# Windowed attention with 64 key columns for 32 queries, values moved by DMA, and half of the rotary sum on VectorE

## The chip, the cores and the metric

The kernel runs on one core of one Trainium2 chip. The metric is the device time of one execution in microseconds. Engines are named TensorE (PE in the profile; PEld is its weight load), VectorE (DVE), ScalarE (ACT), GpSimd (POOL) and SyncE (SP, which here only issues DMAs).

## What is computed

`x` has 32 sequences of 128 tokens with 128 channels. A causal attention with a linear bias (phase A) and a cross attention (phase B) come first; both lie outside the change. Then six layers follow, each a windowed attention and a gated MLP, both on token-shifted input. The attention's core, per layer and for 16 heads of 64:

```python
q = q * cos * scale + rotate_half(q) * sin * scale
k = k * cos * inv + rotate_half(k) * sin * inv
# local_attention, w = 32: a block of 32 queries sees its own and the previous block's keys
bk2, bv2 = (look(bk), look(bv))
mask = (it < jb) | (it > jb + w) | (jb == -1)
sim = jnp.einsum('bhwie,bhwje->bhwij', bq, bk2) * QK_SCALE
attn = jax.nn.softmax(jnp.where(mask, -jnp.finfo(sim.dtype).max, sim), -1)
out = jnp.einsum('bhwij,bhwje->bhwie', attn, bv2)
```

A block of 32 queries needs 64 keys, so the first 64 queries need keys 0 to 63, queries 64 to 95 keys 32 to 95, and queries 96 to 127 keys 64 to 127.

## The kernel before

The work of a layer's attention is cut into 128 groups, one for every 4 heads of a sequence. One step of the software pipeline takes in one group at one end and finishes an older one at the other; `LAG`-like numbers in the class `WIN` say how many steps behind its intake each stage of a group runs. Every engine runs a program of its own, written out in order, and waits on semaphores. `windowed` runs steps 5 to 15 of a layer unrolled, bodies 2 to 14 of eight steps (`STEPS`) in a hardware loop, and the last body unrolled. The first five steps (`FILL`) of a layer are laid between the last parts of the previous MLP, and eight drain steps of a layer between the first parts of its MLP.

The stages of a group and who runs them, before the change:

- Step 0: TensorE projects queries and keys (`win_project`, L701, through `split_product`, L698) into `proj_ps` and values (`win_values`, L715) into the upper half of `value_ps`. VectorE multiplies by the rotary tables (`win_cos` L1487, `win_sin` L1495), ScalarE squares (`win_square` L1043), VectorE sums squares (`win_norms` L1502) and clamps (`win_clamp` L1512). GpSimd adds `by_cos` and `by_sin` of queries and keys (`win_rotate` L1206). ScalarE copies the values to `vout` (L1063).
- Every second step GpSimd raises the norms of two groups to the power -1/2 (`win_rnorm` L1214) and, a step later, multiplies both groups' rotated tiles by them (`win_unit` L1226).
- Step 3: TensorE transposes queries and keys (`win_heads` L691), ScalarE copies them to `qk_t` (L1034).
- Step 5: TensorE writes the mask (L730) and adds the scores (`win_scores` L741) in one of two bank pairs, `win_ps`; a head's scores are 128 columns wide. VectorE takes row maxima (`win_max` L1519).
- Step 6: ScalarE takes four exponentials in place, with their row sums (L1052). VectorE takes reciprocals (`win_recip` L1527) and scales the probabilities into `prob` (`win_scale` L1537).
- Step 7: TensorE transposes the probabilities (L757), ScalarE copies them to `prob_t` (L1069), TensorE sums the values (`win_sum_values` L771) into the lower half of `value_ps`. ScalarE's copy to `vout` takes these sums and the new group's values together.
- Step 8: TensorE projects the sums out (L793); VectorE adds every fourth result to `y` (`win_add` L1544).

Every fourth step also brings in a sequence: VectorE's `win_tok` (L1463), TensorE's `win_input` (L672), ScalarE's `xt_high` (L1023) and VectorE's `win_split` to `xt_low` (L1469). The order on each engine within a step, before:

```python
# TensorE: project, turn_probs, values, mask, scores, sum_values, heads, project_out, (input)
# ScalarE: exponentials, copy_probs, square, copy_values, copy_heads, (xt_high)
# VectorE: cos, sin, recip, scale, max, norms, clamp, (tok), (xt_low), (add)
# GpSimd:  rotate, rnorm or unit
```

SyncE issues all DMAs in one order: in each layer the six chunks of `wqkv`, `shift_tokens` of the layer before (two DMAs for each of eight quads of sequences, L507 and L508, which feed the MLP), eight loads of `wo` (L522), then `w1` and `w2`. The MLP's first statistics on VectorE (`mlp_stats`, L1589) stand in the first drain step and wait for the first quad of `shift_tokens`.

## Time and profile before

| what | us |
|---|---|
| median of 3 runs (lowest, highest) | 4208.51 (4206.87, 4213.31) |
| the profiled execution, time | 4210.7 |
| the profiled execution, span | 4208.9 |
| TensorE busy | 3918.9 (93%) |
| VectorE busy | 3703.7 (88%) |
| ScalarE busy | 3550.0 (84%) |
| GpSimd busy | 3379.4 (80%) |
| DMA queue of SyncE, share of 16 engines | 3.3% |

Consecutive instructions of one engine overlap in the timeline: the distance between two starts, here called the pitch, is less than the first one's duration. A wait that an engine had is given in brackets behind the row, with the engine and line that ended it. The granted clock of TensorE over the span was 0.989 of full speed.

### The profile page before, as it was taken

How to read it: one execution, taken by the hardware profiler on the slowest of the kernel's cores; microseconds unless marked ns; L12 is line 12 of the kernel's file. 1: busy time of each engine (PE TensorE's matmuls, PEld its weight loads, DVE VectorE, ACT ScalarE, POOL GpSimd, SP SyncE). 2: the span in 40 equal slices, each digit the busy share in tenths (PEclk: the TensorE clock that was granted, in tenths of full speed). 3: DMA queues.
4: the chain of work that ended last, by engine and by line, in shares of the span. 5: the costliest groups of instructions: out<-in, count | busy, mean ns of one | idle time of the engine just before them, and what ended most of it. 6: DMA issues, size and time to landing. Idle time of an engine off the chain costs nothing.

```text
span 4208.9 us, 137255 instructions
## 1 busy us (share of the span) xinstructions
PE 3918.9 (93%) x49504; PEld 3102.0 (74%) x49504; DVE 3703.7 (88%) x8896; ACT 3550.0 (84%) x11595; POOL 3379.4 (80%) x2461
## 2 busy tenths in 40 slices
PE   7998885999999999989999999999899999999998
PEld 5666664777777777777777777777777777777776
DVE  7998887999988999979999889999799998899996
ACT  6888995999977999959999779999599997699995
POOL 4554446999978999969999789999599997799993
PEclk9999997999999999999999999999999999999999
DMA  3000000000000000010000000000100000000001
GB/s 84 0 0 1 0 0 16 3 2 0 0 21 22 5 0 0 1 41 4 2 0 0 15 28 5 0 0 1 41 4 2 0 0 13 15 5 0 0 1 36
DMA packets 81122, 38.89 MB, mean 9 GB/s; under 512 B 60084, under 2 KB 73266, under 8 KB 80946
## 3 DMA queue, kind: packets, MB, share of 16 engines
q1 hardware_dynamic: 80946, 36.56, 3.3%
q8 instruction: 108, 1.77, 0.2%
q14 instruction: 68, 0.56, 0.0%
HBM read 21.92 MB, written 2.10 MB: 6 GB/s over the span
## 4 chain that ended last, share of the span: by engine, by line
ACT 42%; PE 33%; DVE 13%; issue 10%; POOL 2%; ACTq 1%; SPq 0%; DMA 0%; DVEq 0%; POOLq 0%
ACT pair L1052 20%; PE bank L771 12%; ACT prob_t L1069 7%; ACT vout L1063 6%; ACT qk_t L1034 5%; PE bank L691 5%; PE pair L848 4%; PE bank L698 3%; DVE top L1443 3%; PE bank L793 2%; DVE qk_parts L1418 2%; PE bank L864 2%; PE bank L672 1%; DVE by_sin L1411 1%; ACT prob L977 1%
## 5 line engine op out<-in xcount | busy, mean ns | idle before, releaser
L1214 POOL TENSOR_TENSOR rnorm<-norm2g,neg_half 128x16 f32<-128x16 f32 x384 | 1115.3, 2905 | 181.7 <-DVE norm2g L1512 172.4
L1052 ACT ACTIVATE pair<-pair,top 128x128 f32<-128x128 f32 x3072 | 1055.8, 345 | 34.9 <-DVE top L1519 24.2
L1206 POOL TENSOR_TENSOR rotated<-by_cos,by_sin 128x512 f32<-128x512 f32 x768 | 985.8, 1284 | 51.0 <-DVE by_sin L1495 44.4
L1226 POOL TENSOR_TENSOR rotated<-rotated,rnorm 128x512 f32<-128x512 f32 x768 | 785.3, 1043 | 0.5
L698 PE MATMUL bank<-wqkv_high,xt_high 128*128 128x512 f32 (+1 forms) x1536 | 649.5, 423 | 15.9 <-ACT squares L1043 14.5
L1052 ACT ACTIVATION_READ_ACCUMULATOR pair<-pair,top 128x1 f32 x3072 | 652.3, 212 | 0.0
L1487 DVE TENSOR_TENSOR by_cos<-bank,rot_cos 128x512 f32<-128x512 f32 x768 | 529.9, 690 | 108.2 <-PE bank L698 91.5
L1063 ACT ACTIVATE vout<-bank 128x512 f32<-128x512 f32 (+1 forms) x810 | 466.0, 575 | 150.5 <-PE bank L771 145.1
L771 PE MATMUL bank<-prob_t,vout 128*32 128x128 f32 x12288 | 495.2, 279 | 94.0 <-ACT prob_t L1069 56.8
L1537 DVE TENSOR_TENSOR prob<-pair,rsum 128x512 f32<-128x512 f32 x768 | 530.9, 691 | 40.0
L1043 ACT ACTIVATE squares<-bank 128x512 f32<-128x512 f32 x768 | 458.8, 597 | 109.7 <-DVE by_sin L1495 92.0
L1502 DVE TENSOR_REDUCE norm<-squares 128x8 f32<-128x512 f32 x768 | 519.3, 676 | 11.3 <-ACT squares L1043 9.9
L1519 DVE TENSOR_REDUCE top<-pair 128x4 f32<-128x512 f32 x768 | 522.4, 680 | 0.7
L1495 DVE TENSOR_TENSOR by_sin<-bank,sin_now 128x512 f32<-128x512 f32 x768 | 522.4, 680 | 0.0
L698 PE MATMUL bank<-wqkv_low,xt_high 128*128 128x512 f32 (+1 forms) x1536 | 520.6, 339 | 0.0
L698 PE MATMUL bank<-wqkv_high,xt_low 128*128 128x512 f32 (+1 forms) x1536 | 520.1, 339 | 0.0
L1196 POOL TENSOR_TENSOR kz_parts<-qk_parts,cst 128x512 fp32r<-128x512 f32 x256 | 266.2, 1040 | 307.4 <-DVE qk_parts L1418 307.4
L691 PE MATMUL bank<-cst,rotated 128*128 128x128 f32 x3072 | 504.3, 287 | 2.7 <-POOL rotated L1226 2.5
L1069 ACT ACTIVATE prob_t<-bank 128x512 f32<-128x512 f32 x768 | 474.3, 618 | 4.8 <-PE bank L757 4.8
L793 PE MATMUL bank<-wo_sb,vout 128*128 128x128 f32 x3072 | 472.8, 276 | 2.0 <-ACT vout L1063 2.0
L771 PEld LDWEIGHTS bank<-prob_t,vout 128*32 128x32 f32 x12288 | 289.8, 109 | 239.6 <-ACT prob_t L1069 196.5
L757 PE MATMUL bank<-cst,prob 128*128 128x128 f32 x3072 | 461.8, 273 | 1.4 <-ACT qk_t L1034 1.4
(142 smaller groups left out, 8451.6 us busy)
## 6 DMA issues: line engine op xcount, KB each, us to landing
wqkv_sb<-in_L_ffn_Wqkv_dram SPq DMA_DIRECT2D x36, 256.0 KB, 4.0
ctx_all<-y SPq DMA_DIRECT2D x48, 128.0 KB
ctx_all<-y SPq DMA_DIRECT2D x48, 127.0 KB
wo_sb<-in_L_ffn_Wo_dram SPq DMA_DIRECT2D x48, 64.0 KB, 2.0
out_dram<-y SPq DMA_DIRECT2D x8, 256.0 KB, 3.5
w_sb<-in_L_ffn_W_dram SPq DMA_DIRECT2D x6, 341.0 KB, 3.0
w_sb<-in_L_ffn_W_dram SPq DMA_DIRECT2D x12, 64.0 KB
cst<-in_constants_dram SPq DMA_DIRECT2D x1, 582.0 KB, 3.9
```

The lines of the kernel that those rows point to most:

```text
L691: last = nc.tensor.transpose(turned_ps(it)[:, k * P:(k + 1) * P], flat[:, k * P:(k + 1) * P], ident)
L698: last = nc.tensor.matmul(dst, a[slot][:, :], w[:, which, cols], start=(n == 0), stop=(n == 2))
L771: last = nc.tensor.matmul(value_ps[PAD * h:PAD * (h + 1), half * P:(half + 1) * P], vout[jl][:, at:at + PAD], prob_t[jl % 2][:, h % 2 * 2 ...
L793: last = nc.tensor.matmul(acc_ps[:, 0:P], vout[(j - 1) % STEPS][:, half * P:(half + 1) * P], wo_sb[:, k * P:(k + 1) * P], start=(k == 0), ...
L1052: last = nc.scalar.activation(at, at, ACT.Exp, bias=top[jl % 2][:, h:h + 1], accum_out=psum_raw[jl % 2][:, h:h + 1])
L1063: nc.scalar.activation(vout[j][:, cols], value_ps[:, cols], ACT.Copy).then_inc(c_vout, 1)
L1069: nc.scalar.activation(prob_t[(j - WIN.probs) % 2][:, :, :].rearrange("k h q -> k (h q)"), turn_c_ps[:, :], ACT.Copy).then_inc(c_pt, 1)
L1206: nc.gpsimd.tensor_tensor(rotated[j % 4][:, :, :, :], by_cos[j % 2][:, :, :, :], by_sin[j % 2][:, :, :, :], ALU.add).then_inc(c_rot, 1)
L1214: nc.gpsimd.tensor_tensor(rnorm[slot][:, :, :].rearrange("t g n -> t (g n)"), norm2g[slot][:, :, :].rearrange("t g n -> t (g n)"), neg_hal ...
L1226: nc.gpsimd.tensor_tensor(at, at, rnorm[slot][:, i, :].unsqueeze(2).to_broadcast([P, 2 * HG, DH]), ALU.mult).then_inc(c_unit, 1)
L1487: nc.vector.tensor_tensor(by_cos[j % 2][:, :, :, :], got, table(rot_cos, layer).unsqueeze(2).to_broadcast([P, 2, HG, DH]), ALU.mult).then_ ...
L1537: nc.vector.tensor_tensor(prob[jl % 2][:, :, :].rearrange("q (e i) k -> q e i k", e=2), win_ps[jl % 2].rearrange("q e (i k) -> q e i k", i=2),
```

## The change

Keys: the four heads' scores of a group become 64 columns wide instead of 128, with three bases of keys for three blocks of queries, so scores, maxima, exponentials, scaling and transposes work on half the columns (two transposes for four). Value sums run on 64x64 tiles and need values of other tokens in their own half of the partitions; for these SyncE copies parts of `vout` into `vmoved`, four DMAs for every two groups. The transposed probabilities come out in the lower half of `value_ps` and are copied with the values; the sums go into free halves of the score banks and have a copy of their own. VectorE takes over the query half of the rotary sum. The lags `turn` and `exp` change, and the order of the stages on TensorE, ScalarE and VectorE. `wo` is loaded by one DMA, and `wqkv` of the next layer ahead of this layer's moves. Left out of the diff below: the constants of the mask, semaphores, and the parts of the drain and of the first steps that follow the new order.

```diff
+    turn = 4
     scores = 5
     top = 5
-    exp = 6
+    exp = 5
     scale = 6
     probs = 7
     value = 7
     out = 8
+KEYS = 2 * PAD
+BASES = (0, PAD, 2 * PAD)
...
-        win_ps = [t[:, :].rearrange("q (e n) -> q e n", e=2)[:, :, 0:2 * P] for t in (pair45, pair12)]
+        win_ps, sum_ps = [[t[:, :].rearrange("q (e n) -> q e n", e=2)[:, :, at:at + P] for t in (pair45, pair12)] for at in (0, P)]
...
+            def move_values(l, it, pair):
+                j = 2 * pair + 1
+                sp.wait_ge(c_vout, l * VOUTS + it * STEPS + j + 1)
+                if has(it * STEPS + j - STEPS):
+                    sp.wait_ge(c_value, l * GROUPS + it * STEPS + j - STEPS + 1)
+                elif l:
+                    sp.wait_ge(c_value, l * GROUPS)
+                for i, n, base in ((0, 0, BASES[1]), (0, 1, BASES[2]), (1, 0, BASES[0]), (1, 1, BASES[1])):
+                    sp.dma_start(vmoved[pair][i * KEYS:(i + 1) * KEYS, :, n, :],
+                                 vout_all[base:base + KEYS, 2 * pair:2 * pair + 2, (2 + i) * P:(3 + i) * P]).then_inc(c_moved[pair], 16)
+            def move_body(l, it, first=0):
+                for pair in range(first, STEPS // 2):
+                    move_values(l, it, pair)
...
-                for h in range(HG):
-                    for half in range(2):
-                        sp.dma_start(wo_sb[PAD * h:PAD * (h + 1), :].rearrange("r (g s c) -> r g s c", g=NG, s=2)[:, :, half, :],
-                                     wo[l].rearrange("(g h s r) c -> h s r g c", g=NG, h=HG, r=PAD)[h, half]).then_inc(s_wo_in, 16)
+                sp.dma_start(wo_sb[:, :].rearrange("r (k c) -> r k c", c=P), wo[l].rearrange("(k r) c -> r k c", r=P)).then_inc(s_wo_in, 16)
...
+                if l:
+                    for pair in range(2):
+                        move_values(l, 0, pair)
...
+                if l + 1 < DEPTH:
+                    load_wqkv(l + 1)
+                move_layer(l)
...
                     flat = rotated[jl % 4][:, :, :, :].rearrange("t a h d -> t (a h d)")
                     for k in range(4):
-                        last = nc.tensor.transpose(turned_ps(it)[:, k * P:(k + 1) * P], flat[:, k * P:(k + 1) * P], ident)
+                        if k == 3 and not isinstance(it, int):
+                            sums_ready(layer, it, j)
+                        last = nc.tensor.transpose(heads_ps[:, k * P:(k + 1) * P], flat[:, k * P:(k + 1) * P], ident)
...
                     jl = (j - WIN.scores) % STEPS
                     for i in range(2):
-                        for lower, keys in ((0, slice(0, DH)), (DH, slice(WINDOW, P))):
+                        for lower, n, base in ((0, DH, BASES[0]), (DH, PAD, BASES[1]), (DH + PAD, PAD, BASES[2])):
                             for e in range(2):
-                                rows, q0, k0 = slice(e * DH, (e + 1) * DH), i * P + lower, (2 + i) * P
-                                last = nc.tensor.matmul(win_ps[jl % 2][lower:lower + DH, e, i * P + keys.start:i * P + keys.stop],
-                                                        qk_t[jl % 4][rows, q0:q0 + DH], qk_t[jl % 4][rows, k0 + keys.start:k0 + keys.stop],
+                                rows, q0, k0 = slice(e * DH, (e + 1) * DH), i * P + lower, (2 + i) * P + base
+                                last = nc.tensor.matmul(win_ps[jl % 2][lower:lower + n, e, i * KEYS:(i + 1) * KEYS],
+                                                        qk_t[jl % 4][rows, q0:q0 + n], qk_t[jl % 4][rows, k0:k0 + KEYS],
                                                         start=False, stop=False, skip_group_check=True, tile_position=(e * DH, lower))
...
-                    for h in range(HG):
-                        last = nc.tensor.transpose(turn_c_ps[:, h * P:(h + 1) * P], prob[jl % 2][:, h, :], ident)
+                    for e in range(2):
+                        last = nc.tensor.transpose(value_ps[:, e * P:(e + 1) * P], prob[jl % 2][:, e, :], ident)
                     last.then_inc(c_pturn, 1)
...
+            def sums_ready(layer, it, j):
+                if here(it, j, WIN.value):
+                    jl = (j - WIN.value) % STEPS
+                    if jl % 2 == 0:
+                        pe.wait_ge(c_moved[jl // 2], 64 * (layer * ENDED + it + (1 if j >= WIN.value else 0)))
+                    if here(it, j, WIN.scale):
+                        pe.wait_ge(c_scaled, layer * GROUPS + it * STEPS + j - WIN.scale + 1)
+                    pe.wait_ge(c_vout, layer * VOUTS + it * STEPS + j + 1)
...
                 if here(it, j, WIN.value):
...
-                    for half in range(2):
-                        for h in range(HG):
-                            at = 2 * P + h * DH + half * PAD
-                            last = nc.tensor.matmul(value_ps[PAD * h:PAD * (h + 1), half * P:(half + 1) * P],
-                                                    vout[jl][:, at:at + PAD], prob_t[jl % 2][:, h % 2 * 2 + h // 2, :],
-                                                    start=True, stop=True, tile_position=(0, PAD * h))
+                    if isinstance(it, int):
+                        sums_ready(layer, it, j)
+                    for n, (lower, width) in enumerate(((0, DH), (DH, PAD), (DH + PAD, PAD))):
+                        for e in range(2):
+                            for i in range(2):
+                                rows = slice(i * KEYS, (i + 1) * KEYS)
+                                out_ps = last_sum_ps[i] if last_sum(it, j) else sum_ps[(j - WIN.scale) % 2][:, i, :]
+                                last = nc.tensor.matmul(out_ps[e * DH:(e + 1) * DH, lower:lower + width], values_of(j, i, e, n),
+                                                        vout[j][rows, e * P + lower:e * P + lower + width],
+                                                        start=True, stop=True, tile_position=(i * KEYS, e * DH))
...
+                    pe.wait_ge(c_sum, m + 1)
+                    for i in range(2):
+                        k = 2 * (jl % NG) + i
+                        last = nc.tensor.matmul(acc_ps[:, 0:P], prob_t[(j - 1) % 2][:, i, :], wo_sb[:, k * P:(k + 1) * P],
...
                 win_project(layer, it, j)
                 win_turn_probs(layer, it, j)
                 win_values(layer, it, j)
+                win_project_out(layer, it, j)
+                win_heads(layer, it, j)
                 win_mask(layer, it, j)
                 win_scores(layer, it, j)
                 win_sum_values(layer, it, j)
-                win_heads(layer, it, j)
-                win_project_out(layer, it, j)
...
-                        at = win_ps[jl % 2][:, h // 2, h % 2 * P:(h % 2 + 1) * P]
+                        at = win_ps[jl % 2][:, h // 2, h % 2 * KEYS:(h % 2 + 1) * KEYS]
...
             def win_copy_values(layer, it, j):
-                fresh, summed = here(it, j, 0), here(it, j, WIN.value)
-                if fresh or summed:
+                fresh, turned = here(it, j, 0), here(it, j, WIN.probs)
+                if fresh or turned:
+                    if turned:
+                        act.wait_ge(c_pturn, layer * GROUPS + it * STEPS + j - WIN.probs + 1)
                     if fresh:
                         act.wait_ge(c_vproj, layer * GROUPS + it * STEPS + j + 1)
-                    if summed:
-                        act.wait_ge(c_value, layer * GROUPS + it * STEPS + j - WIN.value + 1)
-                    cols = slice(0 if summed else 2 * P, 4 * P if fresh else 2 * P)
+                    cols = slice(0 if turned else 2 * P, 4 * P if fresh else 2 * P)
...
-            def win_copy_probs(layer, it, j):
-                if here(it, j, WIN.probs):
-                    m = layer * GROUPS + it * STEPS + j - WIN.probs
-                    act.wait_ge(c_pturn, m + 1)
-                    nc.scalar.activation(prob_t[(j - WIN.probs) % 2][:, :, :].rearrange("k h q -> k (h q)"), turn_c_ps[:, :], ACT.Copy).then_inc(c_pt, 1)
+            def win_copy_sums(layer, it, j):
+                if here(it, j, WIN.value):
+                    act.wait_ge(c_value, layer * GROUPS + it * STEPS + j - WIN.value + 1)
...
+                    else:
+                        last = nc.scalar.activation(prob_t[j % 2][:, 0:2, :], sum_ps[(j - WIN.scale) % 2], ACT.Copy)
+                    last.then_inc(c_sum, 1)
             def win_copies(layer, it, j):
-                win_exponentials(layer, it, j)
-                win_copy_probs(layer, it, j)
-                win_square(layer, it, j)
                 win_copy_values(layer, it, j)
                 win_copy_heads(layer, it, j)
+                win_square(layer, it, j)
+                win_exponentials(layer, it, j)
+                win_copy_sums(layer, it, j)
...
@@ -1203,7 +1261,7 @@
                     if has(it * STEPS + j - 4):
                         pool.wait_ge(c_heads, g - 3)
-                    nc.gpsimd.tensor_tensor(rotated[j % 4][:, :, :, :], by_cos[j % 2][:, :, :, :], by_sin[j % 2][:, :, :, :], ALU.add).then_inc(c_rot, 1)
+                    nc.gpsimd.tensor_tensor(rotated[j % 4][:, 1, :, :], by_cos[j % 2][:, 1, :, :], by_sin[j % 2][:, 1, :, :], ALU.add).then_inc(c_rot, 1)
             def win_rnorm(layer, it, j):
...
                     rows = lambda b: b[:, :, :, :].rearrange("t a h (s d) -> t (a h) s d", s=2)
                     nc.vector.tensor_tensor(rows(by_sin[j % 2]), got, rows(sin_now), ALU.mult).then_inc(c_sin, 1)
+            def win_rotate_queries(layer, it, j):
+                if here(it, j, 0):
+                    g = layer * GROUPS + it * STEPS + j
+                    dve.wait_ge(c_sin, g + 1)
+                    if has(it * STEPS + j - 4):
+                        dve.wait_ge(c_heads, g - 3)
+                    nc.vector.tensor_tensor(rotated[j % 4][:, 0, :, :], by_cos[j % 2][:, 0, :, :], by_sin[j % 2][:, 0, :, :], ALU.add).then_inc(c_qrot, 1)
             def win_norms(layer, it, j):
...
@@ -1534,8 +1602,8 @@
                     if has(it * STEPS + j - WIN.scale - 2):
                         dve.wait_ge(c_pturn, m - 1)
-                    nc.vector.tensor_tensor(prob[jl % 2][:, :, :].rearrange("q (e i) k -> q e i k", e=2), win_ps[jl % 2].rearrange("q e (i k) -> q e i k", i=2),
-                                            rsum[jl % 2][:, :].rearrange("q (e i) -> q e i", e=2).unsqueeze(3).to_broadcast([P, 2, 2, P]), ALU.mult).then_inc(c_scaled, 1)
+                    nc.vector.tensor_tensor(prob[jl % 2][:, 0:2, :].rearrange("q e (i k) -> q e i k", i=2), win_ps[jl % 2].rearrange("q e (i k) -> q e i k", i=2),
+                                            rsum[jl % 2][:, :].rearrange("q (e i) -> q e i", e=2).unsqueeze(3).to_broadcast([P, 2, 2, KEYS]), ALU.mult).then_inc(c_scaled, 1)
             def win_add(layer, it, j):
                 if j % NG == 3 and here(it, j, WIN.out + NG - 1):
@@ -1544,10 +1612,11 @@
                     nc.vector.tensor_tensor(seq(y, b), seq(y, b), acc_ps[:, 0:P], ALU.add).then_inc(c_yadd, 1)
             def win_step(layer, it, j):
+                win_recip(layer, it, j)
+                win_scale(layer, it, j)
                 win_cos(layer, it, j)
                 win_sin(layer, it, j)
-                win_recip(layer, it, j)
-                win_scale(layer, it, j)
+                win_rotate_queries(layer, it, j)
                 win_max(layer, it, j)
...
```

## Rows read from the trace of the kernel before

**Rows 1.** Chain of waits that ended last, share of the span by line.

```profile
ACT pair L1052 20%; PE bank L771 12%; ACT prob_t L1069 7%; ACT vout L1063 6%; ACT qk_t L1034 5%; PE bank L691 5%; PE pair L848 4%; PE bank L698 3%; DVE top L1443 3%; PE bank L793 2%; DVE qk_parts L1418 2%; PE bank L864 2%; PE bank L672 1%; 
```

**Rows 2.** Timeline, ScalarE and TensorE, one step: start us, us, engine line operation.

```profile
1507.39 0.60 ACT L1063 ACTIVATE vout<-bank 128x512 f32<-128x512 f32 x1 [0.19 <-PE bank L771]
...
1508.38 0.34 ACT L1052 ACTIVATE pair<-pair,top 128x128 f32<-128x128 f32 x1
...
1509.65 0.22 ACT L1052 ACTIVATION_READ_ACCUMULATOR pair<-pair,top 128x1 f32 x1
...
1509.75 0.62 ACT L1069 ACTIVATE prob_t<-bank 128x512 f32<-128x512 f32 x1
...
1510.42 0.65 PE L771 MATMUL bank<-prob_t,vout 128*32 128x128 f32 x16
...
1511.19 0.60 ACT L1063 ACTIVATE vout<-bank 128x512 f32<-128x512 f32 x1 [0.23 <-PE bank L771]
```

**Rows 3.** Timeline, VectorE, the same step.

```profile
1507.89 0.68 DVE L1502 TENSOR_REDUCE norm<-squares 128x8 f32<-128x512 f32 x1
...
1508.68 0.17 DVE L1512 TENSOR_REDUCE norm2g<-norm 128x8 f32<-128x16 f32 x1
...
1509.03 0.69 DVE L1487 TENSOR_TENSOR by_cos<-bank,rot_cos 128x512 f32<-128x512 f32 x1 [0.18 <-PE bank L698]
...
1509.64 0.68 DVE L1495 TENSOR_TENSOR by_sin<-bank,sin_now 128x512 f32<-128x512 f32 x1
...
1510.24 0.17 DVE L1527 RECIPROCAL rsum<-psum_raw 128x4 f32<-128x4 f32 x1
...
1510.44 0.69 DVE L1537 TENSOR_TENSOR prob<-pair,rsum 128x512 f32<-128x512 f32 x1
...
1511.05 0.68 DVE L1519 TENSOR_REDUCE top<-pair 128x4 f32<-128x512 f32 x1
```

**Rows 4.** Timeline, VectorE, `by_cos` eight steps apart.

```profile
1513.40 0.69 DVE L1487 TENSOR_TENSOR by_cos<-bank,rot_cos 128x512 f32<-128x512 f32 x1
...
1545.07 0.69 DVE L1487 TENSOR_TENSOR by_cos<-bank,rot_cos 128x512 f32<-128x512 f32 x1
```

**Rows 5.** Groups by line and shape: busy us, mean ns, idle before.

```profile
L1206 POOL TENSOR_TENSOR rotated<-by_cos,by_sin 128x512 f32<-128x512 f32 x768 | 985.8, 1284 | 51.0 <-DVE by_sin L1495 44.4
...
L1063 ACT ACTIVATE vout<-bank 128x512 f32<-128x512 f32 x726 | 433.5, 597 | 150.5 <-PE bank L771 145.1
...
L1063 ACT ACTIVATE vout<-bank 128x256 f32<-128x256 f32 x84 | 32.4, 386 | 0.0
```

**Rows 6.** Timeline, VectorE, a step with a new input.

```profile
1512.82 0.29 DVE L1469 TENSOR_TENSOR xt_low<-bank,xt_high 128x128 fp32r<-128x128 f32 x1 [0.30 <-ACT xt_high L1023]
```

**Rows 7.** Timeline, VectorE, two reciprocals in the drain of layer 0.

```profile
1201.80 0.18 DVE L1527 RECIPROCAL rsum<-psum_raw 128x4 f32<-128x4 f32 x1
...
1204.87 0.18 DVE L1527 RECIPROCAL rsum<-psum_raw 128x4 f32<-128x4 f32 x1
```

**Rows 8.** Timeline, VectorE and GpSimd overlapping, at three places.

```profile
28.27 1.04 POOL L1196 TENSOR_TENSOR kz_parts<-qk_parts,cst 128x512 fp32r<-128x512 f32 x1 [4.07 <-DVE qk_parts L1418]
28.62 0.83 DVE L1411 SCALAR_TENSOR_TENSOR by_sin<-by_cos,cst 128x128 fp32r<-128x128 f32 x1 [0.43 <-ACT by_cos L961]
...
1283.64 2.91 POOL L1214 TENSOR_TENSOR rnorm<-norm2g,neg_half 128x16 f32<-128x16 f32 x1 [1.82 <-DVE norm2g L1512]
...
1284.33 0.68 DVE L1570 TENSOR_TENSOR y<-y,b_sb 128x512 f32<-128x512 f32 x1
...
1290.13 0.68 DVE L1570 TENSOR_TENSOR y<-y,b_sb 128x512 f32<-128x512 f32 x1
...
1290.29 1.65 POOL L1206 TENSOR_TENSOR rotated<-by_cos,by_sin 128x512 f32<-128x512 f32 x1
```

**Rows 9.** SyncE's issues of line 522, 1250 to 1265 us: ns min/median/max; landing.

```profile
L522 SPq DMA_DIRECT2D wo_sb<-in_L_ffn_Wo_dram x8: 422/433/6453, 1251.7 to 1261.0; - x8
...
DMA to landing us min/median/max: 2.0/2.0/8.1
```

97 lines of the change are left out of this document (54 added, 43 removed).

## The prediction

> **What bounds the kernel now.** I read the chain of waits first, then a timeline of one step, because four engines work side by side and no busy share says which of them waits. The chain [rows 1] is ScalarE's and TensorE's: exponentials (L1052), sums of values (L771), copies of probabilities, values and heads (L1069, L1063, L1034). The timeline [rows 2] shows how one step closes on itself: exponentials start at 1508.38, the copy `prob_t` 1.37 us later at 1509.75, TensorE's value sums at 1510.42 wait for it, the copy `vout` at 1511.19 waits for them (idle 0.23), and one step earlier `vout` came at 1507.39: 3.80 us. Summed: 1.37 + 0.62 + 0.05 + 0.65 + 0.12, then two copies in (1508.38 - 1507.39) = 0.99, makes 3.80. The loop holds TensorE's sums and all of ScalarE except its squares, which lie in the hole. VectorE [rows 3] is nearly as full, but waits for nobody's result in a chain of its own: exponentials there belong to the step before.
>
> Over eight steps `by_cos` goes from 1513.40 to 1545.07 [rows 4]: 31.67 us, 3.96 each. Eight times 3.80 is 30.40; the rest, 1.27, falls on the two steps of the eight in which a next input passes (`xt_high`, then `xt_low`), 0.63 each. 768 groups are worked; the first five of each layer lie beside the MLP, so 738 steps pay 3.96 us, about 2922 us of the profiled 4210.7.
>
> **What it removes.** TensorE: the sums' wait for `prob_t`, and two of four transposes. ScalarE: two `vout` forms, 0.597 at 512 columns and 0.386 at 256 [rows 5], give 0.82 ns a column. So an exponential with 64 columns for 128 falls 0.05, from a pitch of 0.34 (three pitches between 1508.38 and the last accumulator read, less its 0.25) to 0.29; the 256-column copy of sums saves 0.21 against `prob_t`. ScalarE's pitches become 4 x 0.29 + 0.30 + 3 x 0.50 = 2.96 us. GpSimd: half the columns of a 1.28 us sum [rows 5], at most 0.64 and at least nothing if its cost were all fixed; I take 0.5, so 0.8 is left. The old loop is cut; what is next?
>
> **VectorE.** A 512-column instruction lasts 0.68 to 0.69 and the next starts 0.60 after it [rows 3]; one of 128 columns lasts 0.29 [rows 6]. Linear between: 256 columns last 0.42, pitch 0.34. Scaling and maximum save 0.26 each, the new query sum adds 0.34. It also waits for `by_sin` of its own engine. Bounds for that gap: 0.03 (reciprocal 1510.24 + 0.17 to scaling 1510.44) and 0.11 (norm 1507.89 + 0.68 to clamp 1508.68) [rows 3]; I take 0.08, nearer the second, which also waits twice. So by_sin to query sum is 0.76 instead of a pitch of 0.60. VectorE alone: 0.20 + 0.34 + 0.60 + 0.76 + 0.34 + 0.34 + 0.76 + 0.10, with 0.16 for the three small instructions of every fourth step, 3.60.
>
> **The new wait.** The exponentials move from one step after their maximum into the same step, while reciprocal and scaling move to the head of VectorE's next step. Then everything is in one line: maximum(s), exponentials(s), reciprocal(s+1), scaling, by_cos, by_sin, query sum, maximum(s+1). Its length: maximum 0.42, hop 0.04, exponentials 3 x 0.29 + 0.20 + 0.22 = 1.29, hop 0.04, reciprocal to scaling 0.20, scaling 0.34, by_cos 0.60, by_sin with the gap 0.76, query sum 0.34: 4.03 us. Norm and clamp (0.86) hide beside the exponentials, so VectorE idles 0.5 a step. Behind it wait by_cos and with it all of the next step. The method can be tried on the old drain, which has just this line without rotations: 0.20 + 0.60 + 0.68 + 1.49 + two hops is 3.05; the reciprocals lie 3.07 apart [rows 7].
>
> Every fourth step is longer. ScalarE's input copy stands behind exponentials and sum copy, and VectorE's `xt_low` and output addition wait for it ahead of the next reciprocal: 4 x 0.29 + 0.04 + 0.30 + 0.28 + 0.03, then two pitches of 0.21, is 2.23 (0.30 and 0.28 are copies of 256 and 128 columns by rows 5, the first as a pitch, 0.21 is 0.29 less the same overlap) from the first exponential to the reciprocal, against 1.33 otherwise: I take +0.86, since the copy's start may overlap. Today `xt_low` follows `xt_high` likewise [rows 6], but ahead of the exponentials. Mean step 4.03 + 0.86 / 4 = 4.24.
>
> Cost: (4.24 - 3.96) x 738 = +207 us.
>
> **TensorE, GpSimd, DMA.** Scores and sums go from 16 to 24 small instructions each. Sixteen of the sums last 0.65, their last result's latency included [rows 2]: at most 0.04 apiece, 16 more at most 0.65, at least nothing, if a shorter one issues faster (half the columns). I take 0.02 apiece, +0.3, against -0.2 for two transposes and the prob_t wait that goes; TensorE stays under 4.0, and hides. At the upper bound it needs 3.80 + 0.65 - 0.2 = 4.25, hardly over the new mean. GpSimd fits the present 3.96 and only loses work, so it fits 4.24. Its new wait for the query sum comes a step early and is hidden. The four moves of each pair of steps (128 runs of 512 B each) resemble an old `wo` load with the same runs: 0.43 us of SyncE's queue by the median, and (1261.0 - 1251.7) / 7 = 1.33 from issue to issue, one long stall included [rows 9]. That is 1.7 to 5.3 us of 8.5, a landing takes 2.0 [rows 9], and the values are used five steps later: hidden. But the moves now stand ahead of shift_tokens on SyncE. After the last values copy come 4 moves, two shift DMAs and a landing: 6 x 0.43 + 2.0 = 4.6 us, or 6 x 1.33 + 2.0 = 10.0. Until the statistics in the drain there are a step and three instructions (4.03 + 0.88) less the 0.8 by which, as an estimate, that copy lies behind its step's reciprocal: 4.1. I take +1 us a layer, nearer the median issue, up to +5. In the drain the line shrinks from 3.07 by 0.7 where nothing else stands: 3 steps a layer. Together +6 - 13 = -7. The eight `wo` loads made one, weights loaded a layer ahead and waits on `c_sum` have their cover in the MLP: nothing.
>
> **Sum**: 4210.7 + 207 - 7 = 4410.7 in a profiled execution; that stands 2.2 over the median of the three runs, 4208.5. Forecast 4408.
>
> **The shared port.** A row shows it: at 28.62 a VectorE instruction with two SBUF inputs of 128 columns takes 0.83, where such a width costs about 0.3, and ends 0.14 after GpSimd's product of 1.04 is over. At 1290.13 the reverse: VectorE started 0.16 earlier, keeps its 0.68, and GpSimd's sum takes 1.65 instead of 1.28 [rows 5, 8]. At 1284.33 a power under way for 0.69 holds nobody up [rows 8]. The new query sum has two SBUF inputs. By my order it meets a power on even steps; on odd ones GpSimd's key sum waits for the same `by_sin`. I expect VectorE first, since it needs no hop. The Trainium skill ("SBUF — State Buffer", Who interferes with whom) says that a VectorE instruction with two SBUF inputs contends with a GpSimd one that reads SBUF, and that whichever issues first blocks the other fully. By that rule, the 1284.33 row should have been blocked too, and every even step with it; the trace disagrees there, at least once the power has read its small inputs.
>
> **Rivals.** (a) GpSimd gets the port first, on odd steps. The query sum then waits out a sum of 0.8, and its own line moves by about that: +0.4 a step, +295 us, 4703. For it: both are released by the same event. Against: the 0.16 lead in the rows. Chance 0.12. (b) Faster. Place: VectorE between maximum and reciprocal. If the exponentials fit under norm and clamp, only VectorE's own sum of 3.60 is left: -0.36 x 738 = -266, 3943. It decides at the exponentials' pitch: 0.22 breaks even ((4.24 - 3.96) / 4 = 0.07 below 0.29), 0.15 gives all of it. For it: four engines lose work and the old loop is truly gone. Against: the fixed part of an exponential, 0.34 - 0.11 = 0.23 already, doesn't shrink with columns. Chance 0.12, most of it near the break-even. (c) The change doesn't lengthen the line as I say, because gaps and pitches sum to a little less and TensorE's relief is felt on fourth steps: 3.96 to 4.07 a step, 4200 to 4290. Chance 0.09. (d) SyncE's queue binds: 4 moves over 8.5 us a pair, needing 2.1 us each, above every issue in rows 9 but the stalled one; at 2.4 us each the step is 4.8, +620 us, 4828. Chance 0.03.
>
> **Numbers.** The forecast has 0.64. Its own range follows from the bounds: gap 0.03 to 0.11 (-37 to +22 us), exponentials' pitch 0.27 to 0.31 (-60 to +60), fourth-step detour 0.5 to 1.0 (-66 to +26), drain and DMA -10 to +30: 4300 to 4520. To leave out no more than 2 in 10, the range takes most of (c): 4275 to 4530. What a measurement can tell from no change is about 0.2%, 8.4 us. Faster: (b) without a sliver, 0.11. Same: 0.03 out of (b) and (c). Slower: the rest, 0.86.
>
> **What would show it.** Right: by_cos to by_cos 4.0 on three steps and 4.8 to 4.9 on the fourth; VectorE idle before the reciprocal (L1527) some 0.5 us a step, put down to the exponentials; ScalarE idle before its exponentials, released by the maximum; in the chain, VectorE's share up and TensorE's down; the exponential's mean 0.29. Wrong: reciprocals without idle time, steps below 3.96; query sums of 0.8 or more instead of 0.42 (a); waits for moved values on TensorE, or SyncE's issues over 1.5 us (d).

## The result, and the profile after

The changed kernel takes 4682.91 us (median of 4 runs, 4679.10 to 4686.16), against 4208.93 for the kernel before on the same chip: a ratio of 1.1124, 95% interval 1.1105 to 1.1144, so 474 us slower. The forecast was 4408 in a range up to 4530: the sign was right, the size was not. The profiled execution has a span of 4684.4 us; TensorE is busy for 4212.9 us (90%), VectorE 3681.5 (79%), ScalarE 3240.9 (69%), GpSimd 3109.8 (66%). Every engine but TensorE has less to do than before; TensorE has 294 us more. In the steps compared here the granted clock is 1.00 in both kernels. Its mean over the span is lower after the change (0.984 against 0.989), because it falls to half more often around the ends and starts of the layers; what that costs is part of the drain's figure below and was not separated. Of x8_heads_first below only one execution counts: the other took 14880.81 us at a granted clock of 0.212.

The chain of waits of the changed kernel, by engine and by line, stands where [rows 1] stood:

```profile
PE 40%; ACT 28%; DVE 22%; issue 8%; DVEq 1%; POOL 1%; SPq 0%; DMA 0%; ACTq 0%; POOLq 0%
ACT pair L1104 19%; PE pair L776 13%; PE bank L843 11%; DVE top L1587 7%; PE bank L728 6%; ACT prob_t L1124 6%; PE pair L899 3%; PE pair L765 3%; DVE top L1502 2%; DVE qk_parts L1477 2%; DVE by_cos L1546 1%; DVE by_sin L1554 1%; PE bank L915 1%; DVE by_sin L1470 1%; ACT prob L1029 1%
```

L1104 is the exponentials, L776 the scores, L843 project_out, L1587 the maximum, L728 the heads, L1124 the copy of sums. VectorE's rotary products (L1546, L1554), which the forecast line runs through, have 1% each. The sign that the prediction named, VectorE's share up and TensorE's down, came true by half: VectorE's went from 13% to 22%, TensorE's from 33% to 40%. Distances of `by_cos` give the steps: 36.40 us for eight, 4.55 each, where [rows 4] had 3.96. Ordinary steps take 4.17 to 4.34, the two with an input 5.20 and 5.59. (4.55 - 3.96) x 738 is 435 of the 474 us.

One step of the changed kernel in its timeline (line 776 is the scores), with the order of [rows 2]:

```profile
1602.00 0.29 ACT L1104 ACTIVATE pair<-pair,top 128x64 f32<-128x64 f32 x1 [0.45 <-DVE top L1587]
...
1603.08 0.21 ACT L1104 ACTIVATION_READ_ACCUMULATOR pair<-pair,top 128x1 f32 x1
...
1603.18 0.39 ACT L1124 ACTIVATE prob_t<-pair 128x256 f32<-128x256 f32 x1
1603.33 0.18 DVE L1595 RECIPROCAL rsum<-psum_raw 128x4 f32<-128x4 f32 x1 [0.47 <-ACT pair L1104]
...
1603.62 0.71 PE L843 MATMUL bank<-wo_sb,prob_t 128*128 128x128 f32 x4 [0.20 <-ACT prob_t L1124]
...
1604.17 0.60 PE L728 MATMUL bank<-cst,rotated 128*128 128x128 f32 x4
...
1604.70 0.25 PE L765 MATMUL pair<-band_b,ident_b 64*64 64x128 bf16 x4
...
1604.78 1.03 PE L776 MATMUL pair<-qk_t 64*64 64x64 f32 x24
...
1605.19 0.42 DVE L1563 TENSOR_TENSOR rotated<-by_cos,by_sin 128x256 f32<-128x256 f32 x1
1605.24 0.97 POOL L1264 TENSOR_TENSOR rotated<-by_cos,by_sin 128x256 f32<-128x256 f32 x1 [1.12 <-DVE by_sin L1554]
...
1605.88 0.42 DVE L1587 TENSOR_REDUCE top<-pair 128x4 f32<-128x256 f32 x1 [0.26 <-PE pair L776]
...
1606.34 0.29 ACT L1104 ACTIVATE pair<-pair,top 128x64 f32<-128x64 f32 x1 [0.45 <-DVE top L1587]
...
1608.10 0.29 DVE L1528 TENSOR_TENSOR xt_low<-bank,xt_high 128x128 fp32r<-128x128 f32 x1 [1.00 <-ACT xt_high L1075]
1608.32 0.29 DVE L1612 TENSOR_TENSOR y<-y,bank 128x128 f32 x1
...
1608.83 0.71 PE L843 MATMUL bank<-wo_sb,prob_t 128*128 128x128 f32 x4 [0.70 <-DVE y L1612]
```

A ring, that is, a chain of waits that comes back to its own start one step later, is to be seen that the prediction did not list: exponentials to the copy of sums, which stands behind them on ScalarE (1.18), copy to project_out (0.44), to heads (0.55), to the mask (0.53), to the scores (0.08), to the maximum (1.10), to the next exponentials (0.46): 4.34 us. The maximum waits 0.26 for the scores, so VectorE's own line is not the last one. The last three rows belong to the next step, one with an input. TensorE itself was busy for 4.14 of the 4.34 us from 1602.00 to 1606.34, where before the change it was busy for 3.73 of 3.80 (1517.14 to 1520.94). The waits of the changed kernel (us in total, times, longest) say the same, and that the exponentials wait for the maximum in each group:

```profile
ACT pair L1104 <- DVE top L1587: 390.1, 768, 7.8
...
PEld bank L843 <- ACT prob_t L1124: 304.7, 641, 1.2
DVE rsum L1595 <- ACT pair L1104: 230.3, 564, 0.6
...
DVE xt_low L1528 <- ACT xt_high L1075: 178.5, 180, 1.7
DVE top L1587 <- PE pair L776: 159.7, 493, 2.6
...
PE bank L843 <- DVE y L1612: 102.4, 168, 0.8
...
DVE stats L1658 <- DMA ctx_all<-y: 70.2, 30, 7.7
```

The scores take 1.03 us for 24 instructions; in the kernel before, 16 took half of that:

```profile
1505.91 0.30 PE L730 MATMUL pair<-band_b,ident_b 64*64 64x256 bf16 x4
1506.05 0.50 PE L741 MATMUL pair<-qk_t 64*64 64x64 f32 x16
```

The new ones alternate: for either head pair first 64x64 tiles, then 64x32 tiles for the blocks of 32 queries. Mask and sums on either side of them are 64x64, so the tile form changes four times a step. The value sums also went from 16 to 24 instructions and got no dearer: from the first sum to the next stage 0.48 us pass (1605.74 to 1606.22), where before it were 0.57 (1506.62 to 1507.19).

### The profile page after: what moved, and what is told of

The parts are those of the page before. It is cut to its first block, busy times and chain, and to the rows that moved or that the text cites. A ratio compares the mean times of both kernels' runs of the same rounds, so it can differ in the third digit from the quotient of the medians.

```text
span 4684.4 us, 162974 instructions
## 1 busy us (share of the span) xinstructions
PE 4212.9 (90%) x60256; PEld 3257.4 (70%) x60256; DVE 3681.5 (79%) x9664; ACT 3240.9 (69%) x11601; POOL 3109.8 (66%) x2461
## 4 chain that ended last, share of the span: by engine, by line
PE 40%; ACT 28%; DVE 22%; issue 8%; DVEq 1%; POOL 1%; SPq 0%; DMA 0%; ACTq 0%; POOLq 0%
ACT pair L1104 19%; PE pair L776 13%; PE bank L843 11%; DVE top L1587 7%; PE bank L728 6%; ACT prob_t L1124 6%; PE pair L899 3%; PE pair L765 3%; DVE top L1502 2%; DVE qk_parts L1477 2%; DVE by_cos L1546 1%; DVE by_sin L1554 1%; PE bank L915 1%; DVE by_sin L1470 1%; ACT prob L1029 1%
## 5 line engine op out<-in xcount | busy, mean ns | idle before, releaser
L1104 ACT ACTIVATE pair<-pair,top 128x64 f32<-128x64 f32 x3072 | 879.1, 286 | 390.1 <-DVE top L1587 390.1
L1264 POOL TENSOR_TENSOR rotated<-by_cos,by_sin 128x256 f32<-128x256 f32 x768 | 696.7, 907 | 567.4 <-DVE by_sin L1554 563.4
L1086 ACT ACTIVATE qk_t<-bank 128x512 f32<-128x512 f32 x768 | 459.2, 598 | 606.9 <-PE bank L728 606.6
L776 PE MATMUL pair<-qk_t 64*32 64x64 f32 (+1 forms) x18432 | 798.5, 230 | 0.0
L843 PE MATMUL bank<-wo_sb,prob_t 128*128 128x128 f32 x3072 | 548.8, 302 | 240.7 <-ACT prob_t L1124 131.2
L843 PEld LDWEIGHTS bank<-wo_sb,prob_t 128*128 128x128 f32 x3072 | 403.8, 191 | 398.2 <-ACT prob_t L1124 304.7
L776 PEld LDWEIGHTS pair<-qk_t 64*32 64x32 f32 (+1 forms) x18432 | 538.6, 114 | 175.5 <-issue 1.4
L1104 ACT ACTIVATION_READ_ACCUMULATOR pair<-pair,top 128x1 f32 x3072 | 625.7, 204 | 0.0
L1546 DVE TENSOR_TENSOR by_cos<-bank,rot_cos 128x512 f32<-128x512 f32 x768 | 522.7, 681 | 6.2 <-PE bank L735 6.1
L1554 DVE TENSOR_TENSOR by_sin<-bank,sin_now 128x512 f32<-128x512 f32 x768 | 522.8, 681 | 0.0
L1115 ACT ACTIVATE vout_all<-bank 128x512 f32<-128x512 f32 (+1 forms) x810 | 468.0, 578 | 76.1 <-PE bank L735 58.3
L728 PE MATMUL bank<-cst,rotated 128*128 128x128 f32 x3072 | 469.0, 276 | 0.0
L1587 DVE TENSOR_REDUCE top<-pair 128x4 f32<-128x256 f32 x768 | 325.7, 424 | 177.8 <-PE pair L776 159.7
L823 PE MATMUL pair<-vout_all 64*64 64x64 f32 x6096 | 423.0, 232 | 33.7 <-issue 33.7
```

The source lines that it names most:

```text
L728: last = nc.tensor.transpose(heads_ps[:, k * P:(k + 1) * P], flat[:, k * P:(k + 1) * P], ident)
L776: last = nc.tensor.matmul(win_ps[jl % 2][lower:lower + n, e, i * KEYS:(i + 1) * KEYS], qk_t[jl % 4][rows, q0:q0 + n], qk_t[jl % 4][rows, k ...
L843: last = nc.tensor.matmul(acc_ps[:, 0:P], prob_t[(j - 1) % 2][:, i, :], wo_sb[:, k * P:(k + 1) * P], start=(k == 0), stop=(k == 2 * NG - 1))
L1104: last = nc.scalar.activation(at, at, ACT.Exp, bias=top[jl % 2][:, h:h + 1], accum_out=psum_raw[jl % 2][:, h:h + 1])
L1264: nc.gpsimd.tensor_tensor(rotated[j % 4][:, 1, :, :], by_cos[j % 2][:, 1, :, :], by_sin[j % 2][:, 1, :, :], ALU.add).then_inc(c_rot, 1)
L1546: nc.vector.tensor_tensor(by_cos[j % 2][:, :, :, :], got, table(rot_cos, layer).unsqueeze(2).to_broadcast([P, 2, HG, DH]), ALU.mult).then_ ...
```

## The experiments

All are edits of the changed kernel. "Eight steps" is from `by_cos` to the eighth after it, in the layer around 1500 us, where the changed kernel has 36.40. Each ratio is to the kernel before on the same chip as that run (medians 4208.87 to 4213.43), and the change itself was measured on one chip only, so a difference of a few us between two versions says nothing.

**x1_form_order: the scores sorted by tile form.** Same 24 matmuls, two form changes a step instead of four.

```diff
-                    for i in range(2):
-                        for lower, n, base in ((0, DH, BASES[0]), (DH, PAD, BASES[1]), (DH + PAD, PAD, BASES[2])):
+                    for blocks in (((0, DH, BASES[0]),), ((DH, PAD, BASES[1]), (DH + PAD, PAD, BASES[2]))):
+                        for i, (lower, n, base) in [(i, block) for i in range(2) for block in blocks]:
```

> The changed kernel with the scores' small matmuls put in another order: first the 64x64 ones of both sequences halves, then the 64x32 ones, so the form of the tile changes once within the scores instead of three times. Theory F (a line through TensorE bounds the step: exponentials, copy of sums, output projection, heads, mask, scores, maximum, 4.33 us; and each change of form costs some 0.2 us): the scores shrink from 1.03 to about 0.6, the step falls until VectorE's own line of 4.03 to 4.07 binds, about -0.3 on 738 steps, 4450 to 4490 us. Rival R1 (every small matmul costs 0.04 us whatever its form): scores stay at 1.0, 4683 within 10. Rival R2 (VectorE's line bounds already): scores shrink, time stays at 4683 within 10.

4524.22 us, ratio 1.0747 (1.0716 to 1.0778); eight steps 34.67, ordinary ones 3.98 to 4.17, most of them 4.06 to 4.08. The scores take 0.76 (timeline), and the chain changes hands:

```profile
DVE 50%; ACT 26%; issue 13%; PE 9%; DVEq 1%; POOL 0%; SPq 0%; ACTq 0%; DMA 0%; POOLq 0%
ACT pair L1104 20%; DVE by_cos L1546 11%; DVE by_sin L1554 10%; DVE top L1587 7%; DVE rotated L1563 6%; PE pair L899 4%; DVE rsum L1595 3%; DVE top L1502 3%; DVE qk_parts L1477 2%; PE bank L915 1%; ACT prob_t L1124 1%; DVE by_sin L1470 1%; DVE ctx_all L1673 1%; ACT prob L1029 1%; DVE prob L1605 1%
```

Two form changes fewer are 0.27 us of scores and 159 us of the whole. What then binds is the line of the prediction, at 4.07 where it had 4.03. The ring, shorter by 0.27, would be 4.07 as well; that VectorE's line is the later one follows from the chain and from the maximum's waits for the scores, which fall from 159.7 us (493 times) to 23.6 (20 times).

**x9_more_forms: the suspected cost doubled.** The loop over the two halves `e` goes outside the loop over the three blocks: eight form changes a step, the same 24 matmuls.

> The scores of one half of a head pair after the other: 64x64, 64x32, 64x64, 64x32 for each of the two halves and key sets, so that the tile form changes 8 times a step between mask and sums instead of 4 times, with the same 24 matmuls. Theory (a change of form costs 0.14 to 0.2 us, read from the starts in the changed kernel, and the scores lie in the line that binds): 4 more changes cost 0.56 to 0.8 us a step, times 738 is +410 to +590, 5095 to 5275 us. Rival (the scores are dear because they are 24 small instructions, whatever their form): same count, so no change, 4670 to 4695. A smaller rise, up to 4800, would say that the neighbours on the two row halves used to overlap and no longer do.

5405.51 us, ratio 1.2834 (1.2812 to 1.2855), 723 above the change; eight steps 43.7 (from 1601.09 us on). (5.46 - 4.55) x 738 is 672 of these; in the rest the granted clock may have a part: its mean is 0.968 against 0.984, and between 1500 and 1510 us it is 0.60. The ends of the scores in its timeline, mask and first sum beside them:

```profile
1601.56 0.25 PE L765 MATMUL pair<-band_b,ident_b 64*64 64x128 bf16 x4
1601.64 1.97 PE L776 MATMUL pair<-qk_t 64*64 64x64 f32 x24
1603.54 0.27 PE L823 MATMUL pair<-vout_all 64*64 64x64 f32 x1
```

0.76, 1.03 and 1.97 us for 2, 4 and 8 changes: 0.14 us a change, then 0.24. The rival, that 24 instructions are dear whatever their form, has fallen. Drawn on to no change at all, the first slope leaves 0.49 us for 24 instructions (an estimate), about what 16 took before the change: the price is the changes' and not the eight more instructions'.

Why the last four cost more can be read from the single instructions of the traces. From the last start in one form to the first in the other, 0.148 us pass on the way to 64x32 and 0.146 on the way back (medians over all layers, nine in ten within 0.001), the same in the changed kernel, in x1 and in x9. Starts within a form lie 0.007 apart or less by the median, and 0.10 at most with few exceptions in the changed kernel. So a change costs the same wherever it stands, and four more are 0.59 of the 0.94. The other 0.35 go with the alternation of the two row halves, which this order takes away: the two 64x64 instructions of a half start 0.107 apart by the median, where in the changed kernel those of the two halves start 0.003 to 0.007 apart. That the scores write at different partitions is not the cause: before the change they did so too, in one form, and 95 of 100 starts followed within 0.08.

**x2_project_last: project_out behind the value sums,** to take it out of the ring.

```diff
-                win_project_out(layer, it, j)
                 win_heads(layer, it, j)
                 win_mask(layer, it, j)
                 win_scores(layer, it, j)
                 win_sum_values(layer, it, j)
+                win_project_out(layer, it, j)
```

A wait for the copy of sums goes ahead of the last heads transpose, since scores and sums share banks.

> The changed kernel with the output projection behind the value sums on TensorE again, and the wait for the copied sums ahead of the last heads' transpose instead of ahead of the projection. Theory F: 0.33 of projection and most of the heads' 0.5 leave the line; what is left of it through TensorE is about 3.6 us, so VectorE's line of 4.03 to 4.07 binds and then VectorE waits for nobody ahead of its maximum: 4430 to 4490 us. R2 (VectorE's line bounds already): 4683 within 10.

4713.84 us, ratio 1.1197 (1.1165 to 1.1230); a miss. The heads now wait for ScalarE's copy of the values (326.1 us, 546 times), and that copy for TensorE's values (331.9 us): another ring, and most ordinary steps take 4.38 to 4.47. What project_out's place is worth by itself this run doesn't tell.

**x8_heads_first: heads ahead of project_out,** the wait for values and scaling moved into project_out's second half.

> The changed kernel with the heads' transposes ahead of the output projection on TensorE, so that they fill the wait for the copied sums; the waits for values, scaling and moves go to the projection's second half. Theory F: heads leave the line through TensorE (4.33 - 0.5 = 3.83), VectorE's line of 4.07 and TensorE's own work of about 4.1 bind: a normal step of 4.05 to 4.15, 4683 - 0.2 x 738 = 4500 to 4550 us. Rival R5 (learnt from the run with the projection last, which got slower: TensorE's own work with the wait for the values copy is a ring of 4.5): 4650 to 4720.

4612.68 us in one execution, so there is no interval; eight steps 35.90. Right in direction, half the size expected. The heads have left the ring, but the wait for the copy of the values, now in project_out's second half, closes another: from 1524.73 exponentials to the copy of sums 1.18, to the copy of values 0.30, to the mask 1.07 (project_out's second half waits for that copy, in all 126.0 us, 468 times), to the scores 0.08, to the maximum 1.10, to the next exponentials 0.46: 4.19 us, and ordinary steps take 4.14 to 4.26. TensorE is busy for nearly all of such a step (4.17 of 4.18 us from 1526.62), so how much of the bound is its own sum can't be told here.

**x4_rotary_gpsimd: the query half back on GpSimd,** `win_rotate_queries` and its wait removed.

> The changed kernel with the query half of the rotary sum back on GpSimd. Theory F: VectorE's line loses 0.34 + 0.16 us but doesn't bind; its maximum waits 0.5 longer for TensorE, time 4683 within 15 us. R2 (VectorE's line bounds): about -0.5 x 738, down to 4330. Rival R3 (the shared SBUF port, two-input sums on VectorE blocked by GpSimd): the time falls by 100 us or more.

4671.40 us, ratio 1.1096 (1.1064 to 1.1129); eight steps 36.36. The maximum's wait for the scores grows to 513.9 us from 159.7: VectorE's time saved turns into waiting. The steps are unchanged and the two intervals overlap (1.1105 to 1.1144 for the change), so the query sum costs nothing here, in VectorE's line or at the port.

**x5_no_moves: no moves by DMA,** unmoved values read in their place.

> The changed kernel without the moves: the value sums read the unmoved values of their own partitions instead (so two thirds of the sums take wrong tokens' values), no DMA and no wait for one. Theory F: the moves are hidden, only the statistics' wait at the start of each layer's drain goes (70 us in all are now put down to that DMA, 26 before): 4683 down to 4630. Rival R4 (131072-byte moves disturb the engines or SyncE's queue binds): 4.33 us a step falls below 4.2 and the time below 4580.

4644.03 us, ratio 1.1031 (1.0999 to 1.1063); eight steps 36.40, unchanged. All of the 39 us lies at the drains: from step 120 of a layer to step 8 of the next it takes 146.6 us for 153.3 (means of five), and behind the last layer 6 us less. (A move is 64 KB, 65536 bytes, half of what the expectation says.) The statistics' wait there:

```profile
DVE stats L1659 <- DMA ctx_all<-y: 26.4, 18, 2.4
```

Before the change it was 26.0, with the moves it is 70.2: 44 us, or 7.3 a layer. Within the steps the moves are hidden.

**x6_add_early: the addition right behind the maximum, `xt_low` a step later,** so that the reciprocal of fourth steps doesn't wait for them.

> The changed kernel with the output addition on VectorE right behind the maximum, and xt_low one step later, behind the scaling, so neither waits for ScalarE's input copy ahead of the reciprocal. Theory F: the excess of every fourth step (5.4 to 5.6 against 4.33, so about 1.2) falls to 0.3 to 0.5; 0.8 / 4 x 738 = 150 us less, 4500 to 4570. Rival R6 (the fourth step's excess is TensorE's input matmuls and ScalarE's copy themselves): 4683 within 30.

4663.61 us, ratio 1.1070 (1.1048 to 1.1092); a miss. Instead of two long steps of eight there are four, of 4.54 to 4.89: the lateness moved. By which of the two new orders (`xt_low` ahead of `by_cos`, the input's turn behind the addition) was not separated; TensorE's turn of the input waits 55.6 us for the addition, in 168 steps.

**v1_three_orders: form order, heads first, query sum behind the maximum.**

> Scores by form, heads ahead of the projection, and the query sum behind the maximum on VectorE. Theory F: VectorE's line falls to 4.07 - 0.5 = 3.6, TensorE's to 3.6, TensorE's own work is some 3.7: a normal step of 3.7 to 3.8, a fourth step 1.2 more, 4683 - 0.55 x 738 = 4280 within 50. If VectorE's line was never near (R2 reversed), the run equals one without the query sum moved, at 4.07 a step: 4450 and more.

4423.14 us, ratio 1.0499 (1.0478 to 1.0520); eight steps 33.72, ordinary ones 3.87 to 4.06. The ring and VectorE's line are shorter, yet it is 140 above what was expected: the chain is now 55% TensorE, and the wait of project_out's second half from x8 is in it (106.3 us, 468 times).

**x10_forms_and_heads: the first two of these alone.**

> Scores ordered by form and heads ahead of project_out, the query sum left where the change has it (ahead of the maximum). Theory (TensorE's line is what these two shorten, VectorE's line of about 4.07 a step is a floor under it): ordinary steps stay at 4.06, the gain over the form order alone can only be on fourth steps, 4480 to 4530 us. Rival (TensorE alone binds, the query sum costs nothing): the same time as with the third edit, 4423.

4485.43 us, ratio 1.0656 (1.0638 to 1.0673); ordinary steps 3.99 to 4.16. The time is as the theory had it: form order gives 159 us, heads first 39 more, and moving the query sum (v1) 62 more, where VectorE's line has begun to bind.

**v2_four_orders: v1 with x6's edit.**

> As the run with three orders changed, with the addition early and xt_low late as well. Theory F: the fourth steps fall by 0.8 too: about 4130 within 60, under the kernel before (4209). If it comes out over 4200, a bound is left that the lines don't show (TensorE's own work over 3.9 a step).

4495.89 us, ratio 1.0670 (1.0652 to 1.0687), 73 slower than v1; a miss again. With x6's edit TensorE's turn of the input waits for the addition, here for 113.4 us in 168 steps; that this is what turns x6's gain of 19 us into a loss is likely and was not tried apart.

**v4_early_input: the next input taken ahead.** On TensorE its turn goes between project_out and mask, on ScalarE `xt_high` ahead of the exponentials.

> The early input alone on the changed kernel. Theory: fourth steps fall from 5.2 to 5.6 to about 4.6 (the 0.3 for the turn and its wait now stand ahead of the scores, in TensorE's line), mean 4.55 to 4.35, 4683 - 150 = 4535 us, 4500 to 4580. Rival (TensorE's line pays all of the turn and the copy now): under 30 us of gain, 4650 to 4685.

4612.18 us, ratio 1.0958 (1.0940 to 1.0977): 71 us, between theory and rival. Long steps fall from 5.20 and 5.59 to 4.89 and 4.70, but ordinary ones don't shrink.

**v3_orders_early_input: v1 and v4 together.**

> The three orders (form order, heads first, query sum behind the maximum) and the next input taken ahead: TensorE turns it between project_out and the mask, ScalarE copies xt_high ahead of its exponentials, VectorE's order stays. Theory (the fourth step is long because xt_high stands behind exponentials and sum copy, and xt_low, addition and reciprocal wait for it): fourth steps fall from 5.0 to 4.4, ordinary ones stay at 3.95, mean 4.215 to 4.06, 4423 - 114 = 4309 us, 4270 to 4350. Rival (the fourth step is long because of TensorE's own work): TensorE's part is the same in sum, 4400 to 4430.

4370.28 us, ratio 1.0383 (1.0366 to 1.0401); eight steps 33.14; the fastest version with the new tiling, still 161 above the kernel before. Long steps are 4.50 and 4.86. An ordinary step of it, in the view of stretches (us; busy us of PE, PEld, DVE, ACT, POOL):

```profile
1573.39:1577.44 4.05, 3.96 (x75) 3.19 (x69) 3.66 (x11) 3.16 (x12) 2.89 (x2) 1.00 0.21 49
```

TensorE is busy for 3.96 of 4.05 us, and 61% of the chain is its. That looks like an engine bound by its own sum, but busy time counts whole durations, and these overlap, so that a start can come late and leave hardly a gap. The rows of that step show a wait inside project_out:

```profile
1573.51 0.29 ACT L1104 ACTIVATE pair<-pair,top 128x64 f32<-128x64 f32 x1 [0.18 <-DVE top L1587]
...
1574.68 0.40 ACT L1124 ACTIVATE prob_t<-pair 128x256 f32<-128x256 f32 x1
...
1574.98 0.60 ACT L1115 ACTIVATE vout_all<-bank 128x512 f32<-128x512 f32 x1
...
1575.22 0.95 PE L843 MATMUL bank<-wo_sb,prob_t 128*128 128x128 f32 x4
...
1575.68 0.30 PEld L843 LDWEIGHTS bank<-wo_sb,prob_t 128*128 128x128 f32 x2 [0.26 <-ACT vout_all L1115]
...
1576.10 0.25 PE L763 MATMUL pair<-band_b,ident_b 64*64 64x128 bf16 x4
...
1576.18 0.75 PE L774 MATMUL pair<-qk_t 64*64 64x64 f32 x24
...
1576.87 0.27 PE L821 MATMUL pair<-vout_all 64*64 64x64 f32 x1
...
1577.00 0.42 DVE L1587 TENSOR_REDUCE top<-pair 128x4 f32<-128x256 f32 x1 [0.25 <-PE pair L774]
...
1577.44 0.50 PE L733 MATMUL bank<-wqkv_high,xt_high 128*128 128x512 f32 x1
1577.46 0.29 ACT L1104 ACTIVATE pair<-pair,top 128x64 f32<-128x64 f32 x1
```

It is the ring of x8, with the cheaper scores: 1.17 + 0.30 + 1.12 + 0.08 + 0.82 + 0.46 is 3.95 us from one first exponential to the next. The weights of project_out's second half wait for the copy of the values 624 times, 176.5 us in all, and in this step the second half starts some 0.23 us later than the first half's pitch would have it (an estimate from the starts, 1575.34 and 1575.69, and a pitch of 0.12). No run moved this wait.

Mask and scores take 0.77, sums 0.57. Before, mask and scores took 1506.62 - 1505.91 less the 0.26 that the sums' first weight load waits for `prob_t`: 0.45 us, an estimate. The two transposes saved (0.2) are eaten up by the scores alone.

## Why the prediction was wrong, and where it was right

**The step that failed** is the one on TensorE: "I take 0.02 apiece ... TensorE stays under 4.0, and hides." It failed twice over. First, the price: eight more score instructions and the changes of form cost 1.03 - 0.50 = 0.53 us in the scores alone; the prediction had 0.3 for scores and sums together, against an upper bound of 0.65, and the sums cost nothing more. It knew instructions and their columns, and no row of the kernel before had two tile forms in turn within a stage. TensorE's total was missed with it: 3.80 + 0.3 - 0.2 is 3.9, and it is busy for 4.14 of 4.34 us (with the ends of instructions as the profile models them), above the 4.0 and above VectorE's line; as busy time that is an upper figure. Second, TensorE was judged by this total alone, not by its place in a ring. The new wait of project_out for the copy of sums (in the diff, and priced at nothing as "waits on `c_sum`") puts heads, mask and scores behind ScalarE's exponentials. With scores as before, that ring would be 4.34 - 0.53 = 3.81 and hide under VectorE's 4.03, as forecast; with them, it is 4.34. So price and ring only bind together, which x1 shows by taking away half of the price: the ordinary step falls to 4.07. Ordinary steps of 4.17 to 4.34 for 4.03 are most of what was missed.

**The detour of fourth steps** was mis-sized: +0.86 forecast, 5.20 and 5.59 against about 4.3 measured, +0.9 and +1.3. The part that was foreseen is there (`xt_low` waits 1.00 for `xt_high`, 178.5 us in all). The prediction followed the input's copy along VectorE only; TensorE's project_out waits for the addition to `y`, which clears its bank, too (0.70 at 1608.83, 102.4 us in all by the waits). That this is all of the rest was not shown. Taking only the input ahead is worth 71 us (v4).

Step mean 4.55 for 4.24 is 229 of the 275 us missed. **The drain** is the rest: -7 forecast, about +39 measured (474 - 435). The moves ahead of `shift_tokens` on SyncE cost 44 us of waiting, 7.3 a layer; the prediction had seen the place, bounded it at 5 (its own figures, 10.0 - 4.1, make it 5.9) and taken 1. The whole of the 39 goes with the moves (x5).

**What was right.** The exponentials' mean is 286 ns (0.29). The reciprocals wait for the exponentials 564 times, 0.41 us each (0.5 a step forecast). The line through VectorE is 4.07 once nothing else is longer (x1). The gap from `by_sin` to the query sum is 0.03, the lower bound, for 0.08. The moves are hidden within steps (x5).

**The rivals.** (a), at 4703, comes close to the measured time by a mechanism that didn't occur: the view of one line (ns min/median/max) shows that no query sum was held up.

```profile
L1563 DVE TENSOR_TENSOR rotated<-by_cos,by_sin x768: 424/425/427, 697.8 to 4579.8; 128x256 f32<-128x256 f32 x192
...
L1264 POOL TENSOR_TENSOR rotated<-by_cos,by_sin x768: 723/967/1008, 697.9 to 4579.8; 128x256 f32<-128x256 f32 x192
```

It is GpSimd that is stretched, 0.72 to 0.97, where VectorE starts 0.05 earlier (1605.19 and 1605.24 above); x4 removes the meeting, and its 12 us less are within the intervals. (b) failed at the exponentials' pitch, 0.30 where it needed 0.22, as argued. (c) failed. (d) failed too: no wait of an engine for moved values stands in the waits, and x5 leaves the steps as they were.

**What stays open.** Whether the new tiling could beat the kernel before at all. No version here did. The fastest, v3, is 161 us slower; (33.14 - 31.67) / 8 x 738, 136 us, of these lie in the steps, the rest at the drains, where the statistics wait 75.7 us for 26.0. In the steps the wait of project_out's second half for the copy of the values, 176.5 us in all, is a candidate that the new orders brought in themselves, beside TensorE's own work; no run took either away.

## What to carry to other kernels

When a change adds a wait, follow it through every engine's program order until it closes, and price the ring with the longest plausible duration of each stage; an engine under its total can still bind. Do the same for every wait that a reordering moves: x2 and x8 each took a stage out of one ring and closed another by the wait that went with it. Keep TensorE instructions of one tile form together: cutting a tile to what is needed (64x64 to 64x32) saved columns everywhere else and paid 159 us for the alternation. Work that passes only every fourth step is better placed ahead of the stages that others wait for: moved so on TensorE and ScalarE it gave 71 us (v4), while moving VectorE's share to other steps, with a new wait on TensorE, spread the lateness over four steps (x6).

## What was unexpected of the hardware

A change between 64x64 and 64x32 tiles holds TensorE's next start off by 0.146 to 0.148 us, in every run and at every place, where starts within a form follow each other in 0.007 by the median and seldom in more than 0.10. Two changes fewer are 0.27 us of scores (x1). Losing the alternation of the row halves costs besides: two 64x64 instructions of one half start 0.107 apart, those of the two halves 0.007 or less. The Trainium skill ("TensorEngine Tiling (Array Packing)", Key Properties) says that a change of tiling mode drains TensorE; the trace agrees in kind, and the page gives no price.

The port between VectorE and GpSimd goes to whichever starts first. In the changed kernel VectorE starts first in 569 of 768 query sums and keeps its 0.42, while GpSimd's key sum takes 0.96 to 1.01; x1 is the same. In v3, where the query sum stands behind the maximum, GpSimd's sum is the first of the two in 275 of 768. The query sum is then held up in part of them: it takes 0.41 to 0.78 in 203, and 0.76 to 0.92 in the 72 that reach into GpSimd's next product too. The median of all 768 is still 0.42. One of the 72:

```profile
1602.07 0.73 POOL L1264 TENSOR_TENSOR rotated<-by_cos,by_sin 128x256 f32<-128x256 f32 x1
...
1602.30 0.78 DVE L1563 TENSOR_TENSOR rotated<-by_cos,by_sin 128x256 f32<-128x256 f32 x1
```

The Trainium skill ("SBUF — State Buffer", Who interferes with whom) says of such a pair that issue order decides who blocks, and here the trace agrees both ways. The hold is a little shorter than the whole instruction: the query sum ends 0.28 after GpSimd's, not 0.42. A power is the exception, as in [rows 8]: in the changed kernel one runs from 1598.52 to 1601.43, and the query sum that starts at 1600.86 takes 0.43. In all, 199 of the 768 query sums start under a power that is under way, and none of them takes more than 0.43.
